# Gelu statistics in an AdaLN + FFN kernel: transposes and one sum over channels in place of products with ones

## The reference, cut to what matters

```python
def bitlinear(x, w):                       # w is rounded to -1, 0, 1 times its mean magnitude
    xn = layer_norm(x)                     # over the last axis: mean and variance
    ...
h = bitlinear(x, w_fc)                     # (16, 256, 2048)
h = jax.nn.gelu(h, approximate=False)
return bitlinear(h, w_proj)                # normalises h over its 2048 channels first
```

## Time and profile before

| what | value |
|---|---|
| median of three runs | 1108.74 us (1106.15 to 1109.91) |
| the profiled execution: its own time | 1109.38 us |
| its span, first to last instruction | 1107.5 us |
| PE busy | 1060.1 us (96%) |
| DVE busy | 854.9 us (77%) |
| ACT busy | 804.6 us (73%) |
| POOL busy | 553.8 us (50%) |

### The profile page before, as it was taken

How to read it: one execution, slowest core, us unless ns; L and a number is a source line. 1 busy time by engine, 2 the same in 40 slices (tenths; PEclk the granted TensorE clock), 3 DMA queues, 4 the chain that set the end, 5 groups by cost and what they waited for, 6 DMA issues and landing times.

```text
span 1107.5 us, 24385 instructions
## 1 busy us (share of the span) xinstructions
PE 1060.1 (96%) x9457; PEld 668.5 (60%) x9457; DVE 854.9 (77%) x1614; ACT 804.6 (73%) x1370; POOL 553.8 (50%) x365
## 2 busy tenths in 40 slices
PE   8568899999999999999999999999999999999898
PEld 2234565656666665766666576666656666665665
DVE  4877768787877968788796878878687877877656
ACT  4767686868778685877868586786858687684954
POOL 1832290835638092653819274471917447281613
PEclk9769899999999999999999999999999999999999
DMA  9910303131121313122131312213131311212100
GB/s 339 342 32 15 88 20 78 63 77 59 29 74 44 95 46 78 58 40 63 44 96 44 78 59 52 65 31 94 44 77 59 66 56 37 46 39 58 58 20 20
DMA packets 79521, 77.12 MB, mean 70 GB/s; under 512 B 8624, under 2 KB 59952, under 8 KB 78896
## 3 DMA queue, kind: packets, MB, share of 16 engines
q1 hardware_dynamic: 79408, 75.58, 24.5%
HBM read 41.85 MB, written 8.40 MB: 45 GB/s over the span
## 4 chain that ended last, share of the span: by engine, by line
PE 90%; DVE 4%; ACT 3%; issue 1%; POOL 1%; DMA 1%; SPq 0%; ACTq 0%; DVEq 0%
PE F L950 10%; PE F L951 10%; PE F L783 10%; PE F L785 10%; PE QA L714 4%; PE QA L715 4%; PE QA L716 4%; PE QB L714 3%; PE QB L715 3%; PE QB L716 3%; PE T L996 3%; PE SB L842 2%; PE SA L842 2%; PE PV L859 2%; PE PV L858 2%; PE PV L857 2%
## 5 line engine op out<-in xcount | busy, mean ns | idle before, releaser
L950 PE MATMUL F<-yT_hi,fc_t 128*128 128x256 f16 x1024 | 228.2, 274 | 0.0
L951 PE MATMUL F<-yT_lo,fc_t 128*128 128x256 f16 x1024 | 227.8, 274 | 0.0
L664 POOL TENSOR_TENSOR rqk<-ssq,half 128x16 f32<-128x16 f32 x64 | 194.1, 3038 | 45.7 <-DVE ssq L1476 45.7
L783 PE MATMUL F<-proj_t,hs 128*128 128x512 f16 x512 | 194.6, 380 | 0.0
L785 PE MATMUL F<-proj_t,hs 128*128 128x512 f16 x512 | 194.2, 379 | 0.0
L633 POOL TENSOR_TENSOR acc<-acc,hg 128x512 f32<-128x512 f32 x96 | 150.0, 1562 | 15.7 <-ACT hg L1111 2.8
L1437 DVE SCALAR_TENSOR_TENSOR hs<-hg,g_inv,hs 128x512 f16<-128x512 f32 x128 | 104.8, 819 | 64.8 <-ACT hs L1116 64.7
L633 POOL TENSOR_TENSOR acc<-hg 128x512 f32<-128x512 f32 x16 | 20.3, 1269 | 211.0 <-ACT hg L1111 183.3
L1111 ACT ACTIVATE hg<-F,g_fc 128x512 f32<-128x512 f32 x128 | 87.3, 682 | 46.2 <-PE F L951 46.1
L640 POOL TENSOR_TENSOR acc<-acc,hq 128x512 f32<-128x512 f32 x90 | 114.1, 1267 | 13.4 <-ACT hq L1184 4.8
L627 POOL TENSOR_TENSOR rs<-var,half 128x1 f32<-128x1 f32 x32 | 17.6, 551 | 203.4 <-DVE var L1305 203.4
(11 more groups left out here) (227 smaller groups left out, 2727.0 us busy)
## 6 DMA issues: line engine op xcount, KB each, us to landing
stk<-qkT SPq DMA_DIRECT2D x128, 128.0 KB, 2.4
xtok<-in_x SPq DMA_DIRECT2D x17, 512.0 KB, 3.9
xT_sb<-in_xT SPq DMA_DIRECT2D x16, 512.0 KB, 3.5
stk<-qkT SPq DMA_DIRECT2D x128, 64.0 KB, 2.1
xres<-in_x SPq DMA_DIRECT2D x15, 512.0 KB, 3.6
out<-xres SPq DMA_DIRECT2D x15, 512.0 KB, 2.8
stk<-in_w_emb SPq DMA_DIRECT2D x4, 512.0 KB, 6.9
fc_t<-in_w_qkv SPq DMA_DIRECT2D x2, 1024.0 KB, 11.4
```

The source lines that it names most:

```text
L664: pool.tensor_tensor(rqk[:, n % 2, :], ssq[:, n % 2, :], half[:, :], ALU.pow).then_inc(rqk_r, 1)
L783: pe.matmul(FB[t][:, :], hs[:, 0, k // 2, col:col + P], proj_t[:, k, :], start=(k == 0), stop=False)
L950: pe.matmul(dst, w, yT_hi[:, k, :], start=(k == 0), stop=False)
L951: mm = pe.matmul(dst, w, yT_lo[:, k, :], start=False, stop=(k == KT - 1))
```

## The change

At the stats turn PE no longer multiplies by ones. It transposes the four 128x128 blocks of `accf` into T, which they fill: 4 x 128 columns, tokens on the partitions. DVE then adds over the 128 columns of each block with one `tensor_reduce` into a new tile `st_sum` of 128x4, and the scaling by 1/2048 reads that tile. The scaling waits for the sum, and the sum is now what frees T for piece 3. The instruction that squares the mean waits for the scaling through a new semaphore `st_r`. Nothing else is changed.

```diff
+        st_sum = sb("st_sum", [P, 2 * TT])
...
+        st_r = sem("st_r")
...
                         for s in range(2):
                             for t in range(TT):
-                                mm = pe.matmul(T[:, s * TT + t:s * TT + t + 1], accf[:, s, t * P:(t + 1) * P],
-                                               ones[:, 0:1], start=True, stop=True)
+                                mm = pe.transpose(T[:, (s * TT + t) * P:(s * TT + t + 1) * P],
+                                                  accf[:, s, t * P:(t + 1) * P], ident[:, :])
                         mm.then_inc(turned, 1)
...
                             dve.wait_ge(c_r, nth(ffn - 1, 2, 2))
-                        dve.tensor_scalar(st[:, :, :].rearrange("p s t -> p (s t)"), T[:, 0:2 * TT], 1.0 / F, None,
-                                          ALU.mult).then_inc(unturned, 1)
+                        dve.tensor_reduce(st_sum[:, :], T[:, :].rearrange("p (c n) -> p c n", n=P), AX, ALU.add
+                                          ).then_inc(unturned, 1)
                         dve.wait_ge(unturned, turn(i, ("stats", 0)) + 1)
+                        dve.tensor_scalar(st[:, :, :].rearrange("p s t -> p (s t)"), st_sum[:, :], 1.0 / F, None,
+                                          ALU.mult).then_inc(st_r, 1)
+                        dve.wait_ge(st_r, nth(ffn, 1, 1))
                         dve.tensor_tensor(st2[:, :], st[:, 0, :], st[:, 0, :], ALU.mult).then_inc(st2_r, 1)
```

## The result

The changed kernel takes 1115.31 us in the median of five runs (1114.13 to 1116.89), the kernel before 1107.8 us in the median of five (1106.15 to 1109.91): a ratio of 1.0064 with a 95% interval of 1.0051 to 1.0077 (the two medians alone give 1.0068). It is slower by 0.6%, as forecast: 1116.6 us was predicted in the range 1111 to 1120, and +7.9 us against a measured +7.5 us between the medians. The profiled execution took 1116.69 us with a span of 1114.8 us, 7.3 us over the span before. From the first weight load of the first stats turn to the end of the span it is 950.02 us against 942.48, +7.5 us.

A forecast was written before the change was run, and what follows sets the result against it. PE was taken to bound the kernel, busy 63.87 of 63.94 us, with DVE's unbroken stretch deciding at the change. 14 x 0.62 = +8.7, less 0.8, gave +7.9 us on the median 1108.74: 1116.6 us, range 1111 to 1120.

The forecast's parts named there:

- PE's part: Stats turn on PE: four fp32 products (0.80 us) become four transposes (0.38 us), saving 0.42 us for each image.
- DVE's part: Statistics on DVE: the added sum takes 0.68 us and delays the scaling by 0.71 us, bounds 0.60 and 0.80.
- Scaling from SBUF at 0: Scaling of line 1510 on DVE: reading SBUF instead of PSUM was costed at 0.
- Where the two meet: First period, DVE 0.71 us later and PE 0.42 earlier: head 15's scores load 0.62 us later than before.
- the four places: PE's waits for DVE: T bank 0.11 us, values of head 12, scores of head 15, end of stretch adding nothing.
- The 0.09 us of slack: Head 15's scores waiting for head 13's p_lo: 0.14 us gap, 0.05 of it latency, leaves 0.09 us.
- No catching up: Steady periods: PE has no reserve, so the delay is carried and each period grows from 63.94 to 64.56 us.
- The fourteenth period: Iteration 14, taken as one of fourteen like periods, each 0.62 us longer, +8.7 us in all.
- The last two turns: Stats turns in iterations 15 and 16: DVE's delay is hidden, PE's saving counts, together -0.84 us.
- The first, PE's saving in full: Rival, all sixteen images: PE's 0.42 us counts each time, -6.7 us, 1102.0 us; chance 0.09.
- The second: Rival, DVE's sum at half price (some 0.35 us): delay about as large as saving, 1111.5 us; chance 0.09.
- The third, waits that add up: Rival, later p_lo and T bank waits: another 0.2 to 0.4 us a period, 1119.4 to 1122.2 us; chance 0.06.

The follow-up runs named there:

- the kernel with two sums: Changed kernel with DVE's sum over T done twice, the first result unused: 1124.48 us, ratio 1.0148 to the kernel before.
- the transposes alone: Changed kernel without the sum over 128 channels; DVE scales one column of each transposed block: 1107.02 us, ratio 0.9988 to the kernel before.
- the sum first: Changed kernel with the sum moved on DVE ahead of piece 3's normalisation, into its wait for POOL: 1106.19 us, ratio 0.9976 to the kernel before.
- The small instructions moved later: Changed kernel with scale, square and variance of the statistics moved behind head 13's p_lo: 1112.94 us, ratio 1.0039 to the kernel before.
- the kernel before with two scalings moved: Kernel before with two of the four input scalings moved from head 12 to head 8: 1108.67 us, ratio 1.0002.

## Why the prediction was right

- **PE's part.** 0.42 us saved for each image; measured 0.41 (0.80 to 0.39). Four loads and four matmuls in place of eight of each.
- **DVE's part.** The sum was priced at 0.71 us to the scaling's start; 166.92 to 167.64 is 0.72. The Trainium skill's sentence in "VectorE: DVE Perf Modes" ("The DRAIN you can't avoid"), that a semaphore after each instruction costs nothing extra, would have given 0.60. The trace doesn't agree for a start that needs the result. In the kernel with two sums the second, which doesn't wait for the first, starts 0.60 us after it, and the scaling, which waits for the second, 0.72 us after that (166.52 to 167.24).
- **Scaling from SBUF at 0.** This was slightly off: 0.17 us from the start of the instruction to its end against 0.15, 0.20 against 0.18 to the next. That, the 0.01 us of the line above and the roundings are about the 0.02 us by which the period came out over 64.56.
- **Where the two meet.** Of the four places, the changed trace shows the waits at values of head 12 and at scores of head 15, with the latencies read off before (0.12 and 0.05 us). At the T bank PE waits a little too, and is 0.25 us ahead behind it (167.72 - 164.83 against 168.21 - 165.07), where 0.3 was forecast. The 0.09 us of slack was shown twice from the other side, by the transposes alone and by the sum first: both gain 0.10 and 0.09 us a period.
- **No catching up.** Ten of the thirteen periods from iteration 1's turn to iteration 14's grew by 0.63 to 0.65 us, the other three by 0.48 to 0.69, all thirteen together by 8.12 us. Two sums made the usual period 0.60 us longer still.
- **The fourteenth period.** This term of the sum was mis-sized: +0.62 us was counted between the turns of iterations 14 and 15, and it was +0.27 (57.92 to 58.19). The step that was wrong is that iteration 14 was taken to be like the others. There is no next input left to scale, so in the kernel before DVE waits 0.72 us for PE in this stretch, and the sum fits into that wait:

```profile
999.87 0.21 DVE L1325 RECIPROCAL rden<-PV 128x8 f32<-128x8 f32 x1 [0.72 <-PE PV L859]
```

```profile
1007.69 0.21 DVE L1327 RECIPROCAL rden<-PV 128x8 f32<-128x8 f32 x1
```

  Head 15's scores load 4.61 us after iteration 14's stats turn, before 4.79 us: PE is 0.18 us early there, not 0.62 late. What made the period longer all the same comes in iteration 15. ACT starts its exponential on SA 0.25 us earlier after the turn than before (1049.51 and 1041.88 us), but then waits 0.77 us for PE in place of 0.24, and names no idle time from there to the next stats turn:

```profile
1042.72 0.60 ACT L1133 ACTIVATE p_hi<-SA 128x512 f16<-128x512 f32 x1 [0.24 <-PE PV L859]
```

```profile
1050.87 0.60 ACT L1135 ACTIVATE p_hi<-SA 128x512 f16<-128x512 f32 x1 [0.77 <-PE PV L861]
```

  In both kernels PE has stood 2.34 us a little earlier, waiting for a p_lo of DVE's (until 1038.72 us before, 1046.35 after), and then its granted clock falls to 0.50, the 1.2 GHz level, for a stretch. Before the change that begins 1.5 us after PE's start, after it 0.4 us, and so it falls on other matmuls:

```profile
1040.22:1043.63 3.41, 3.41 (x36) 2.03 (x33) 1.66 (x3) 3.07 (x7) 2.54 (x2) 0.50 0.50 153
```

```profile
1046.76:1050.16 3.40, 3.40 (x22) 1.54 (x21) 1.90 (x3) 3.16 (x6) 3.11 (x3) 0.50 0.47 165
```

  The kernel with two sums has no such stretch in iteration 15, and ACT names no wait at this place. That the clock makes the difference is read from these traces; no run tested it.
- **The last two turns.** From iteration 15's stats turn to iteration 16's the time fell by 0.44 us (42.51 to 42.07), and from there to the end by 0.40 (10.60 to 10.20), the forecast -0.84 together.
- **The sum in all.** From the first turn on: +8.12 us in thirteen periods, then +0.27, -0.44 and -0.40, +7.5 us together. The first turn came 0.24 us earlier, which gives the +7.3 us between the spans. The start differs by up to 4.6 us from one kernel's execution to another's, so that the forecast of +7.9 us came within half a microsecond of the +7.5 between the medians is in part luck. In the trace the 0.4 us between forecast and measurement are the fourteenth period's.

**The rivals.** The first, PE's saving in full, fell in the changed kernel for the reason given, and the point from which it decides was then reached on purpose: with the sum in DVE's idle time and 0.79 us moved out of the stretch each steady period gained 0.41 us. One thing in its wording was too generous to it: even without the sum it would not have come true, since 0.09 us of slack caps the saving at a quarter. The second needed a shorter reduction; all sixteen took 0.678 to 0.690 us. The third, waits that add up, fell too: PE's matmuls are idle 0.50 us in front of the values of head 12 and 0.05 us in front of the scores (second period). Against the kernel before, PE is 0.25 us ahead at piece 3, its first matmul of the values is 0.42 us late (4.93 after the stats turn against 4.51), and the scores load 0.64 us late. That last lateness is what the whole period has, not a sum of the two. The small instructions moved later show it again.

## What to carry to other kernels

An engine that is busy 99.9% of a period can still be unable to use what it is given: before pricing a saving, look at the next instruction of that engine which waits for another one, and take the slack there as the cap. Before pricing an addition, find the last idle time in front of it and the first wait behind it on the other engine; between the two it costs its whole time less that slack, and ahead of the idle time, as long as it fits there, it costs nothing. Read the stretch in every iteration in which the code leaves a piece out, and not only in the usual one: here iteration 14, with no next input to scale, had room for the sum. Where a change loses in this way, move the added work (or anything of equal length) across the idle time before giving the change up: here two edits of position turned +7.5 us into -6.7 us, by the medians.

## What was not expected

The profiled executions differ by up to 4.6 us before the first stats turn (it starts at 162.53 us in the kernel with the small instructions later and at 167.09 in the kernel before with two scalings moved). The move doesn't explain it: without it the turn starts between 162.53 and 165.77 us, with it between 164.55 and 167.09. The periods meanwhile repeat within 0.02 us. The timed runs of one kernel spread by about as much (1106.15 to 1109.91 us for the kernel before), and the record shows with what: of the 43 runs of the kernel before beside the eight experiments, the 14 with a mean granted clock of 0.980 or less took 1108.89 us or more, and the 14 with 0.983 or more 1108.67 us or less. In the trace of the kernel before the clock is at its lower level in several stretches up to 125 us, once in iteration 15 and at the very end, and nowhere else, so the first stage is the likeliest place of the difference; that wasn't tested.
